# The first product of a gated MLP: from fp32 products per 128 tokens to three f32r products per sequence of 256

## The reference

```python
h = shift_token(x)
mu = h.mean(-1, keepdims=True)
var = h.var(-1, keepdims=True)
h = (h - mu) / jnp.sqrt(var + 1e-05) * lg + lb
h = h @ w1 + b1                       # 128 -> 2 x 341
a, g = jnp.split(h, 2, axis=-1)
h = a * jax.nn.gelu(g, approximate=False)
x = x + h @ w2 + b2                   # 341 -> 128
```

## Time and profile before

| | us |
|---|---|
| median of 3 runs (lowest to highest) | 1178.63 (1176.59 to 1178.84) |
| the profiled execution's own time | 1174.67 |
| its span, first to last instruction | 1172.9 |
| outputs of MLP 0 (L1384), first to last | 444.4 to 523.3 |
| outputs of MLP 1 (L1384), first to last | 780.6 to 861.3 |

### The profile page before, as it was taken

The page is one execution under the profiler, slowest core; times in us unless marked ns, Lnnn a source line. Parts: engine busy times, 40 slices in busy tenths (PEclk is TensorE's granted clock), DMA queues, the critical chain, the costliest instruction groups (busy, mean ns, idle before and its releaser), DMA issues.

```text
span 1172.9 us, 33608 instructions
## 1 busy us (share of the span) xinstructions
PE 1088.3 (93%) x11412; PEld 922.1 (79%) x11412; DVE 989.7 (84%) x2339; ACT 924.7 (79%) x2616; POOL 730.6 (62%) x1090
## 2 busy tenths in 40 slices
PE   6899976999999989979999999989989997999996
PEld 3777754888888879967888888888867776799996
DVE  4799968999889858878899889768889997599988
ACT  4898866999999975559999999865578886876672
POOL 4799937777777744437777777634589994444431
PEclk9999989999999999999999999999999999999999
DMA  6000000111111112111112310111000000000000
GB/s 201 22 2 1 2 15 17 29 29 29 29 28 24 24 27 65 34 23 23 30 29 47 83 28 19 31 25 28 17 2 2 3 1 2 6 13 14 15 15 16
DMA packets 62408, 30.79 MB, mean 26 GB/s; under 512 B 46197, under 2 KB 56481, under 8 KB 62242
## 3 DMA queue, kind: packets, MB, share of 16 engines
q1 hardware_dynamic: 59474, 27.15, 9.7%
q10 hardware_dynamic: 2768, 1.51, 0.5%
HBM read 9.77 MB, written 2.10 MB: 10 GB/s over the span
## 4 chain that ended last, share of the span: by engine, by line
PE 63%; DVE 14%; ACT 9%; issue 8%; POOL 4%; DMA 0%; DVEq 0%; ACTq 0%; POOLq 0%
PE m_ps_y L1512 7%; PE a_ps_b L1030 5%; PE a_ps_t L1041 5%; PE a_ps_s L936 5%; PE a_ps_a L963 5%; PE a_ps_t L1005 4%; PE a_ps_qk L920 4%; DVE x_e L692 3%; PE f_ps_y L1299 3%; PE f_ps_g L1310 3%; PE a_ps_qk L921 2%; PE a_ps_qk L922 2%; PE f_ps_a L1317 2%; PE a_ps_s L977 2%; PE m_ps_h L1499 2%
## 5 line engine op out<-in xcount | busy, mean ns | idle before, releaser
L1108 ACT ACTIVATE a_e<-a_ps_s,a_stat 128x128 f32<-128x128 f32 x512 | 226.6, 477 | 3.1 <-DVE a_stat L1177 3.1
L1239 POOL TENSOR_TENSOR a_rot<-a_rot 128x512 f32<-128x512 f32 x64 | 82.7, 1293 | 136.1 <-DVE a_rot L1131 136.1
L1233 POOL TENSOR_TENSOR a_e<-a_e,a_stat 128x1024 f32<-128x1024 f32 x64 | 121.4, 1897 | 5.8 <-DVE a_stat L1156 5.8
L1108 ACT ACTIVATION_READ_ACCUMULATOR a_e<-a_ps_s,a_stat 128x1 f32 x512 | 115.7, 226 | 0.0
L1346 ACT ACTIVATE f_gl<-f_ps_g,vec 128x128 f32<-128x128 f32 (+1 forms) x192 | 55.8, 361 | 58.7 <-PE f_ps_g L1310 58.7
L1227 POOL TENSOR_TENSOR a_rot<-a_rot 128x512 f32<-128x512 f32 x64 | 81.6, 1275 | 18.2 <-DVE a_rot L1131 18.2
L1129 DVE TENSOR_TENSOR a_rot<-a_ps_qk,a_rtab 128x512 f32<-128x512 f32 x128 | 86.9, 679 | 0.0
L1131 DVE TENSOR_TENSOR a_rot<-a_ps_qk,a_rtab 128x512 f32<-128x512 f32 x128 | 86.8, 678 | 0.0
L741 DVE TENSOR_REDUCE x_stat<-x_ps_s 128x16 f32<-128x1024 f32 x64 | 77.1, 1205 | 11.4 <-PE x_ps_s L547 11.3
L1173 DVE TENSOR_REDUCE a_stat<-a_ps_s 128x8 f32<-128x1024 f32 x64 | 77.8, 1215 | 4.7 <-PE a_ps_s L936 4.5
L1166 DVE TENSOR_REDUCE a_stat<-a_sq 128x16 f32<-128x1024 f32 x64 | 78.0, 1218 | 3.5 <-ACT a_sq L1115 2.1
(11 more groups left out here) (204 smaller groups left out, 3644.1 us busy)
## 6 DMA issues: line engine op xcount, KB each, us to landing
a_vx<-a_vt SPq DMA_DIRECT2D x64, 128.0 KB, 2.3
...
```

The source lines that it names most:

```text
L1108: act.activation(self.e[n % 2][:, P * i:P * i + P], ps_s[:, P * i:P * i + P], ACT.Exp, bias=stat[:, 24 + i:25 + i], scale=stat[:, root:roo ...
L1233: p.tensor_tensor(e3, e3, self.stat[n % UNROLL][:, 16:24].unsqueeze(2).broadcast_to([P, 8, P]), ALU.mult)\
L1239: p.tensor_tensor(r, r, self.rot2[:, INNER:], ALU.add).then_inc(self.s_n, 1)
```

## The change

The transposes of the two tiles of a sequence go side by side into one PSUM bank. ACT copies all 256 columns at once into an f32r tile with the norm's scale (hTh), at odd tiles only, and DVE writes what the rounding left (hTl). The weights are split once per layer, at the MLP's step PREP = -6, in the tail of the local attention: ACT writes the rounded part w1h (two copies of 341 columns), POOL the rest w1l (two subtractions). Each of the six chunks of hidden units is then three f32r products over 256 tokens (w1h with hTh, w1l with hTh, w1h with hTl), full 128 rows, with zeros behind the 341st column. The gate chunks are issued one step earlier than the value chunks. The norm's shift leaves the copy: at step s = 3 PE multiplies w1 with it (six fp32 products of one column) and DVE adds the result to the biases in two small adds. Gelu and the product of gate and value are three instructions of 256 columns per sequence, with a wait of their own per chunk. The second product keeps its form and moves from s = n + 7 to s = n + 8. ps_g and ps_a become one tile of two banks each, no longer double-buffered. w1h, w1l and hTh live in the key tile kT[0] of the first cross-attention, the activations in its values vall[0]; POOL clears the pads and sets the ones there before MLP 0.

DVE's order within a step changes to: hTl (odd steps), L274, the products of gate and value (odd steps), L1376 (MLP 1), L261 and L263, L1384 last.

The diff, cut to its core; the lines taken out are those of the functions printed above. Counts in other stages that named the MLP's per-tile semaphores are halved with it.

```diff
@@ -910,7 +911,7 @@
...
+            sp.wait_ge(self.mlp.s_ac, 3 * T // 2)
             load_mlp_weights(sp, self.g, 1)
         if s == 20 and l:
             load_expert_weights(sp, self.g)
@@ -1252,17 +1253,22 @@
     def __init__(self, g):
...
+        self.s_z, self.s_t, self.s_hc, self.s_hl, self.s_g, self.s_a, self.s_y, self.s_yc, self.s_gl, self.s_ac, self.s_up, \
+            self.s_wh, self.s_wl, self.s_bp, self.s_bf = (g.sem(f"f_{i}") for i in (
+                "z", "t", "hc", "hl", "g", "a", "y", "yc", "gl", "ac", "up", "wh", "wl", "bp", "bf"))
         self.s_d = [g.sem(f"f_d{i}") for i in range(UNROLL)]
         self.ln = Norm(g, "f_ln")
-        self.h, self.hn, self.hT = self.many("h", UNROLL, D), self.many("hn", 2, D), self.many("hT", 2, D)
+        self.h, self.hn = self.many("h", UNROLL, D), self.many("hn", 2, D)
+        keys, values = g.kT[0], g.vall[0]
+        self.w1h, self.w1l = keys[:, 0:6 * P], keys[:, 6 * P:12 * P]
+        self.hTh, self.hTl = [keys[:, 12 * P + S * i:12 * P + S * i + S] for i in range(2)], self.many("hTl", 2, S, F32R)
         self.st = self.many("st", 2, 16)
-        self.gl, self.act, self.yo = self.many("gl", 2, 3 * P), self.many("act", 2, 3 * P), self.many("yo", 2, D)
+        self.gl, self.yo = self.many("gl", 2, 3 * S), self.many("yo", 2, D)
+        self.act = [values[:, 3 * S * i:3 * S * i + 3 * S] for i in range(2)]
...
+            pair = lambda label, at: [self.bank(f"{label}{l}_{i}", at + i) for i in range(2)]
+            self.banks.append([pair("ps_x", x), self.bank(f"ps_g{l}", g, 2), self.bank(f"ps_a{l}", a, 2), pair("ps_y", y)])
 
     def sync(self, sp, l, s):
         if s == 0 and not l:
@@ -1274,55 +1280,77 @@
             after(sp, self.ln.s_nm, k - UNROLL + 1)
             load_shifted(sp, self.h, self.s_d, self.g.y, n, k)
 
+    def product(self, pe, dst, c, b, signal):
+
+        at = slice(P * c, P * c + P)
+        pe.matmul(dst, self.w1h[:, at], self.hTh[b % 2][:, :], start=True, stop=False)
+        pe.matmul(dst, self.w1l[:, at], self.hTh[b % 2][:, :], start=False, stop=False)
+        pe.matmul(dst, self.w1h[:, at], self.hTl[b % 2][:, :], start=False, stop=True).then_inc(signal, 1)
+
     def tensor(self, pe, l, s):
...
+        if s == 3:
             pe.wait_ge(g.s_mw, g.n_mw * (l + 1))
+            self.take(pe, l, "x")
+            for i, lo in enumerate((0, HID)):
+                for c, w in enumerate(HCH):
+                    m = pe.matmul(ps_x[1][0:w, S + 3 * i + c:S + 3 * i + c + 1], g.mw1[:, lo + P * c:lo + P * c + w], g.vec[:, 1:2],
+                                  start=True, stop=True)
+            m.then_inc(self.s_bp, 1)
         n = s - 4
         if 0 <= n < T:
-            k, u = T * l + n, n % 2
+            k, u, b = T * l + n, n % 2, n // 2
...
+            after(pe, self.s_hc, T // 2 * l + b - 1)
+            after(pe, self.s_hl, T // 2 * l + b - 1)
+            if n == 2:
+                pe.wait_ge(self.s_bf, 2 * l + 2)
+            pe.transpose(ps_x[b % 2][:, P * u:P * u + P], self.hn[u][:, :], g.ident).then_inc(self.s_t, 1)
+        n = s - 5
+        if 0 <= n < T and n % 2:
+            b, q = n // 2, T // 2 * l + n // 2
+            pe.wait_ge(self.s_hc, q + 1)
+            pe.wait_ge(self.s_hl, q + 1)
+            after(pe, self.s_gl, 3 * q)
+            if b == 0:
+                pe.wait_ge(self.s_wh, 2 * l + 2)
+                pe.wait_ge(self.s_wl, 2 * l + 2)
+                pe.wait_ge(self.s_z, 8)
+                self.take(pe, l, "g")
+            for c in range(3):
+                self.product(pe, ps_g[:, S * c:S * c + S], c, b, self.s_g)
+        n = s - 6
+        if 0 <= n < T and n % 2:
+            b, q = n // 2, T // 2 * l + n // 2
+            after(pe, self.s_ac, 3 * q)
+            if b == 0:
+                self.take(pe, l, "a")
+            for c in range(3):
+                self.product(pe, ps_a[:, S * c:S * c + S], 3 + c, b, self.s_a)
+        n = s - 8
+        if 0 <= n < T:
+            k, u, b = T * l + n, n % 2, n // 2
+            pe.wait_ge(self.s_ac, 3 * (T // 2 * l + b) + 3)
...
+                at = S * c + P * u
+                m = pe.matmul(ps_y[u][:, 0:D], self.act[b % 2][0:w, at:at + P], g.mw2[0:w, D * c:D * c + D],
...
     def scalar(self, act, l, s):
...
+        if s == PREP:
             act.wait_ge(g.s_mw, g.n_mw * (l + 1))
+            act.wait_ge(self.cross.s_up, T)
+            after(act, self.s_a, 3 * T // 2 * l)
+            act.activation(self.w1h[:, 0:HID], g.mw1[:, HID:2 * HID], ACT.Copy).then_inc(self.s_wh, 1)
+            act.activation(self.w1h[:, 3 * P:3 * P + HID], g.mw1[:, 0:HID], ACT.Copy).then_inc(self.s_wh, 1)
         if s == 14 and not l:
             act.wait_ge(self.local.s_y, T)
             act.wait_ge(self.local.s_wr, 1)
@@ -1330,20 +1358,20 @@
...
+        if 0 <= n < T and n % 2:
+            k, b, q = T * l + n, n // 2, T // 2 * l + n // 2
...
+            after(act, self.s_a, 3 * (q - 1))
+            act.activation(self.hTh[b % 2][:, :], ps_x[b % 2][:, 0:S], ACT.Copy, scale=g.vec[:, 0:1]).then_inc(self.s_hc, 1)
...
+        if 0 <= n < T and n % 2:
+            b, q = n // 2, T // 2 * l + n // 2
+            after(act, self.s_ac, 3 * (q - 1))
+            if b == 0:
+                act.wait_ge(self.s_bf, 2 * l + 2)
             for c, w in enumerate(HCH):
-                act.activation(self.gl[u][0:w, P * c:P * c + P], ps_g[u][0:w, P * c:P * c + P], ACT.Gelu,
+                act.wait_ge(self.s_g, 3 * q + max(c, 1) + 1)
+                act.activation(self.gl[b % 2][0:w, S * c:S * c + S], ps_g[0:w, S * c:S * c + S], ACT.Gelu,
                                bias=g.vec[0:w, 5 + c:6 + c]).then_inc(self.s_gl, 1)
         if l and 12 <= s < 16:
             if s == 12:
@@ -1353,28 +1381,46 @@
     def vector(self, v, l, s):
...
+        if s == 3:
...
+            v.wait_ge(self.s_z, 8)
+            v.wait_ge(self.s_bp, l + 1)
+            bias = g.vec[:, 2:8].rearrange("p (i c) -> p i c", c=3)
+            more = ps_x[1][:, S:S + 6].rearrange("p (i c) -> p i c", c=3)
+            for rows, c in ((slice(0, P), slice(0, 2)), (slice(0, HCH[2]), slice(2, 3))):
+                v.tensor_tensor(bias[rows, :, c], more[rows, :, c], bias[rows, :, c], ALU.add).then_inc(self.s_bf, 1)
+            v.wait_ge(self.s_bf, 2 * l + 2)
+        n = s - 4
+        if 0 <= n < T and n % 2:
+            b, q = n // 2, T // 2 * l + n // 2
+            v.wait_ge(self.s_hc, q + 1)
+            after(v, self.s_a, 3 * (q - 1))
+            v.scalar_tensor_tensor(out=self.hTl[b % 2][:, :], in0=ps_x[b % 2][:, 0:S], scalar=g.vec[:, 0:1], in1=self.hTh[b % 2][:, :],
+                                   op0=ALU.mult, op1=ALU.subtract).then_inc(self.s_hl, 1)
...
+        n = s - 6
+        if 0 <= n < T and n % 2:
+            b, q = n // 2, T // 2 * l + n // 2
+            after(v, self.s_y, 2 * (q - 1))
+            for c, w in enumerate(HCH):
+                at = slice(S * c, S * c + S)
+                v.wait_ge(self.s_gl, 3 * q + c + 1)
+                v.wait_ge(self.s_a, 3 * q + max(c, 1) + 1)
+                v.scalar_tensor_tensor(out=self.act[b % 2][0:w, at], in0=ps_a[0:w, at], scalar=g.vec[0:w, 2 + c:3 + c],
+                                       in1=self.gl[b % 2][0:w, at], op0=ALU.add, op1=ALU.mult).then_inc(self.s_ac, 1)
...
+        n = s - 2
+        if 0 <= n < T:
+            k = T * l + n
+            v.wait_ge(self.s_d[n % UNROLL], landed(k))
+            self.ln.stats(v, k, self.st[n % 2], self.h[n % UNROLL][:, :])
         n = s - 8
         if 0 <= n < T:
             v.wait_ge(self.s_y, T * l + n + 1)
@@ -1382,21 +1428,29 @@
...
     def clear(self, p):
...
+
+    def pads(self, p):
+
+        p.wait_ge(self.cross.s_up, T)
         for t in self.act:
-            p.memset(t[64:P, 2 * P:3 * P], 1.0).then_inc(self.s_z, 1)
-        p.wait_ge(self.s_z, 4)
+            p.memset(t[:, 2 * S:3 * S], 1.0).then_inc(self.s_z, 1)
+        for t in (self.w1h, self.w1l):
+            for i in range(2):
+                p.memset(t[:, 3 * P * i + HID:3 * P * i + 3 * P].bitcast(F32), 0.0).then_inc(self.s_z, 1)
 
     def gpsimd(self, p, l, s):
+        if s == PREP:
+            if not l:
+                self.pads(p)
+            after(p, self.s_a, 3 * T // 2 * l)
+            for i, (at, lo) in enumerate(((0, HID), (3 * P, 0))):
+                p.wait_ge(self.s_wh, 2 * l + i + 1)
+                p.tensor_tensor(self.w1l[:, at:at + HID], self.g.mw1[:, lo:lo + HID], self.w1h[:, at:at + HID], ALU.subtract)\
+                    .then_inc(self.s_wl, 1)
         n = s - 2
         if 0 <= n < T:
             self.ln.rstd(p, T * l + n, self.st[n % 2])
```

More of the change, by code:

```diff
@@ L36 @@
 UNROLL = 4
+PREP = -6
 AWAY = -2.0e38
@@ L912, in sync @@
             sp.wait_ge(self.mlp.s_y, T)
-            sp.wait_ge(self.mlp.s_ac, 3 * T)
+            sp.wait_ge(self.mlp.s_ac, 3 * T // 2)
             load_mlp_weights(sp, self.g, 1)
@@ L1355, in vector @@
         ps_x, ps_g, ps_a, ps_y = self.banks[l]
```

(29 more changed lines are left out.)

43 lines of the change are left out of this document (removed).

## The result

The changed kernel takes 1211.22 us (median of 4 runs, 1208.90 to 1214.43); the kernel before, on the same chip, 1178.74 us (4 runs). The ratio is 1.0278, with a 95% interval of 1.0248 to 1.0308: 32.5 us slower. The forecast was 1198.6, with a range of 1187 to 1211, so the direction was right and the size too small. The profiled execution took 1211.76 us, its span 1210.0.

A forecast was written before the change was run, and what follows sets the result against it. Before the change PE was taken to bound MLP 0 and the statistics-root-normalisation ring MLP 1; after it, the ring both. Terms +16.4, +2 and +1.6 sum to +20.0 us on 1178.63: 1198.6 us, range 1187 to 1211.

The forecast's parts named there:

- Part 1: PE in the MLPs: f32r products at 0.127 us each, work per sequence from 4.22 to 3.84 us.
- B: Rival, MLPs: f32r products of 256 columns stream at the fp32 rate, twice 0.111 us; 1206 us, chance 0.06.
- D: Rival, MLPs: POOL leg is covered, so PE bounds MLP 0 and DVE's load MLP 1; 1169 us, chance 0.08.
- C: Rival, MLPs: PE's short idles make the clock fall in part to 1.2 GHz; 1256 us, chance 0.03.
- Part 4: Local attention: splitting the weights on ACT and POOL costs 1 us per layer, +2 us for both.
- Part 2: DVE in the MLPs: three products take 1.17 us where 1.56 stood, hTl adds 0.39; load unchanged.
- Part 3: DVE's order in the MLPs: products inside the ring, 4.81 us per sequence in MLP 0, 5.33 in MLP 1; +16.4 us.
- Part 5: Tail of local attention: DVE waits for PE's products folding the shift into the biases, 0.8 us per layer; +1.6 us.
- Part 6: DMAs, layer 1 weight waits and steps the MLPs share with the next stage: 0, between -2 and +4 us.
- the ring: MLPs: loop of statistics, POOL's root, normalisation, statistics, forecast to bound both after the change; 1198.6 us, chance 0.80.

The follow-up runs named there:

- e7: Changed kernel with each chunk of the first product as one fp32 product of 256 columns instead of three f32r ones: 1212.9 us, ratio 1.0296.
- e1: Changed kernel with DVE's statistics L261 and L263 moved ahead of the three gate and value products: 1185.02 us, ratio 1.0055.
- e2: Kernel before (fp32, one tile per step) with only DVE's list put in the changed kernel's order: 1207.77 us, ratio 1.0243.
- e9: Kernel before with DVE's order normalisation, statistics, products, x update, residual: 1172.14 us, ratio 0.9938.
- e3: Changed kernel with POOL's part of the weight splitting moved behind the softmax scaling of the same step: 1204.17 us, ratio 1.0214.
- e4: Changed kernel without the products, adds and waits that fold the norm's shift into the biases (shift left out of the result): 1211.24 us, ratio 1.0272.
- e8: Changed kernel with both the statistics ahead of the products and POOL's splitting behind the softmax scaling: 1178.63 us, ratio 0.9991.

## Why the prediction was right in kind and wrong in size

**Part 1, PE: right and without effect.** 0.117 us per product, not 0.127; e7 shows that the whole saving bought at most 1.7 us. Rivals B and D fall by the windows and the waits. C falls for the MLPs, where the clock is 1.00; outside them it was part of the loss (Part 4).

**Part 2, DVE's work: right.** The three products take 840.80 - 839.63 = 1.17 us, hTl 0.48 in its row and 0.40 to the next start in e1 (483.28 to 483.68).

**Part 3, the order: right.** Distances of 4.82 and 5.36 us against 4.81 and 5.33, +18.0 us in the loops against +16.4. The remainder is MLP 0: 12.5 x 4.82 = 60.3 leaves 4.1 us for POOL's and the weights' side jobs, where I had 2.6. e1 and e2 show it from both sides: the order alone costs 29 us on the old kernel, and one move of it returns 26 on the new, some of which is a gain over the old order (e9).

**Part 4, the splitting: the step that failed.** "Free if all falls into POOL's idle third, 3.5 us per layer if none does. I take 1, since POOL's gap of some 2 us per tile is about its size." I compared the work with the size of the gap and not with its place. POOL executes its list in order; the pieces were ahead of the scaling that PE waits for, and the gap lay behind it. The price was 4.0 and 4.1 us in the long step of each layer and 7.0 us in all by e3, against 2 forecast. Two things were wrong in the step. First, the overlap: nothing of the work fell into the gap, POOL came 3.7 us late, half of it a wait for ACT's copies that the sum had named but not priced, and PE waited 2.4 us. Second, the clock was put at no cost: after this idle it fell to 0.50 for 3.4 us in both layers, which is 1.6 of the 4.0 us in layer 0 by the comparison with e4. The row on which the clock was forecast, 418 to 430 us at 1.00, ends exactly where a fall begins in the trace of the kernel before:

```profile
430.00:433.40 3.40, 2.96 (x37) 2.85 (x38) 0.94 (x3) 0.73 (x2) 1.68 (x1) 0.50 0.03 7
```

The prediction had named "local attention longer by more than 3 us per layer (part 4)" as a sign that it was wrong, and this sign came.

**Part 5, the biases: +1.6 forecast.** The medians of e4 cannot tell it from 0; the traces give about 1.4 in all at an equal clock. Nothing here speaks against the forecast.

**Part 6: 0 forecast, +4.1.** I called the steps shared with the next stage paced by it "at 3 us and more per step, above the ring". They grew by 1.9 and 2.1 us, and in e1 and e8 these fall back (22.9 and 22.7 against 23.3 before in MLP 0, 25.8 and 26.1 against 25.4 in MLP 1): so the order is needed for the growth. It is not enough: e2 has an even longer ring, and its shared steps take 23.7 and 26.0. Ring and sequence form together make the 4 us. The earlier trace rows had no row on these steps one by one; a mean of 3 us hides single steps of about 1 us, in which a ring of 5.36 us per sequence can be the longer one. It was within the bound that I gave (+4).

With the measured sizes, the loops, the splitting and the shared steps are 18.0 + 7.0 + 4.1 = 29.1 of the 32.5 us. Of the rest, 1.9 us lie between local attention and MLP 1's first output (52.3 against 50.4). The same stretch is 52.2 us in e8 and e4, 51.9 in e2, 51.5 in e1 and 50.4 in e9. So it is neither the biases nor the splitting's place; the new order lengthens it without the sequence form (e2), and the sequence form without the new order (e1, e8). Which wait it is I did not settle. The 2.5 us behind MLP 1 were forecast as 0 and are open too. The forecast missed because several terms were small in the same direction, the splitting by the most (5 to 6 us), not because the ring was wrong.

**What the f32r form itself is worth.** e8 and e9 have the same order on DVE, and e9 is 6.5 us faster. By their traces the 25 steps of MLP 0 take 57.1 us in e8 and 54.7 in e9, the 23 of MLP 1 51.8 and 50.0, and the 1.9 us ahead of MLP 1 are e8's alone. A sequence without side jobs is short in e8: 4.15 us in MLP 1, which is DVE's odd step and the bare ring, and 4.0 in MLP 0, where DVE waits 0.33 us for ACT's copy ahead of hTl and 0.16 for PE, against 2 x 2.11 = 4.22 in e9. So taking work from PE could give at most 0.1 to 0.2 us per sequence before something else binds. More than that is lost around it: over MLP 0 DVE waits in e8 3.6 us for ACT's copies and 1.9 for PE, in e9 0.7 for ACT and nothing for PE, while the waits for loads are alike (2.9 and 3.4). Which part of the 6.5 us each of them makes no run separates.
